# Vision layer on one core: the first two pairs' grey picture summed on VectorE, first transfers divided over two queues, set-up placed later

## The chip, the core and the metric

One core of a Trainium2 chip runs the whole program. The metric is device time in microseconds (us) of one execution. TensorE (PE) does matmuls, VectorE (DVE) and ScalarE (ACT) do elementwise work, GpSimd (POOL) here does little but issue accumulating DMAs, and SyncE (SP) only issues DMAs. Matrices are float32. The profile gives the clock that was granted to TensorE; 1.00 is 2.4 GHz and 0.50 is 1.2 GHz.

## The reference, cut to what matters

64 colour images of 256 x 256 are turned to grey, convolved with two 3 x 3 Scharr filters, and go through one RWKV attention layer (256 channels, 256 time steps) and a layer of 8 experts.

```python
gray = einsum('bchw,c->bhw', x, (0.2989, 0.587, 0.114))
h = (abs(conv(gray, sx)) + abs(conv(gray, sy))) / 2       # padding SAME
n = layernorm(h)                                          # rows are time steps
k, v, r = (mix(n, tm_i) @ W_i.T for i in 'kvr')           # mix: n and n one step before
h = h + (sigmoid(r) * wkv(w, u, k, v)) @ Wo.T             # wkv: a scan over 256 steps
h = h + top1_expert(layernorm(h), Wg, W1, b1, W2, b2)
```

## The kernel before, in words

The images go in 32 pairs through six stages, LOAD, GRAY, EDGE, WKV, PROJ, FFN. Step n of every engine's program holds stage s of pair n - s, so that six pairs are under way. Steps 0 to 7 are written out, a loop of four steps a turn does those from 8 to 31, and steps 32 to 36 drain. Each engine runs its own list in order and waits on semaphores.

The way of a pair to its first matmul is through DRAM. In LOAD, SP brings red and green to `planes` (four DMAs of 256 KB, L265) and copies blue from DRAM to DRAM into `gray_dram` (two DMAs, L273). In GRAY, ACT scales red and green in place (`scaled`, L784), and POOL adds them to `gray_dram` with accumulating DMAs, red first (L405), then green (L411), with a wait for red between. SP waits for green and then loads `rows_in` (ten DMAs, 1.6 MB: for each of two images three shifted copies of the rows on 32 partitions each, L329, and two border rows of 3 partitions each, L335). In EDGE, PE convolves `rows_in` with `conv_w` in four groups (`convolve(0)` to `(3)`, L1002), ACT takes absolute values (L776), DVE sums them (L511) and makes the statistics, ACT normalises (L875), PE transposes (L1096), DVE makes the differences and `mixed_k`, `mixed_v` (L557). In WKV of the next step PE projects to k, v, r (L1008), and DVE and ACT run the scans.

There is one `rows_in`, two `planes`, two images' worth of `gray_dram` for each of two pairs. SP's list in step n is: `planes` of pair n (after green of pair n - 2 has been added), wait for the four convolutions of pair n - 2, blue of pair n, wait for green of pair n - 1, `rows_in` of pair n - 1, then the results of pair n - 5.

PE's list in a step begins with `convolve(0)`, `convolve(1)`, `project_k(0)`, `convolve(2)`, `convolve(3)`, `project_k(1)`. `convolve(2)` waits for the first absolute value of its own pair, since they share a bank. ACT's list in a step begins with the two `scaled` of the next pair, then the absolute values.

Set-up stands ahead of and between the first steps: SP zeroes all of `gray_dram` (1 MB), loads the filter `scharr_dj`, eight small parameter arrays and Wk, Wv, Wr before it loads the first blue; PE transposes parameters and these weights before the first convolution; DVE prepares the first expert layer (`setup_experts`) just ahead of its step 2, the other weights ahead of its step 3.

## Time and profile before

| | us |
|---|---|
| three runs, median | 1195.4 |
| lowest and highest | 1194.34, 1196.62 |
| the profiled execution, its own time | 1192.23 |
| its span | 1190.7 |
| PE busy | 1109.3 (93%) |
| DVE busy | 1003.7 (84%) |
| ACT busy | 858.2 (72%) |

The span runs from the first instruction to the last. A busy share is a mean over stages: here the first stretch and the last differ from the long middle. Rows of the timeline give the start of a merged group, its length, the engine, the line, and in brackets the idle time of the engine ahead of it and what ended that. `SPq` and POOL rows of DMAs are issues, not the movement of data. A view with DMA landings counts from issue to landing.

### The profile page before, as it was taken

The page shows a single profiled execution, that of the slowest core. Times are in us where ns is not written, and L with a number is a line of the kernel's source. Part 1 is how long each engine was busy: PE and PEld are TensorE (multiplying, and loading weights), DVE is VectorE, ACT ScalarE, POOL GpSimd, SP SyncE. Part 2 cuts the span into 40 slices and gives each one's busy share as a digit, 9 for nine tenths or more (in the row PEclk, how much of TensorE's full clock was granted, in tenths as well). Part 3 has the DMA queues.
Part 4 walks back from the last instruction along what each step waited for, and adds up shares of the span by engine and source line. Part 5 has one row for each costly group of instructions (what it writes and reads, how often), then busy time and mean ns, then how long its engine had stood idle before and what let it go on. Part 6 is the DMA issues. An engine that isn't in the chain of part 4 may idle for free.

```text
span 1190.7 us, 16854 instructions
## 1 busy us (share of the span) xinstructions
PE 1109.3 (93%) x5571; PEld 696.7 (59%) x5571; DVE 1003.7 (84%) x1828; ACT 858.2 (72%) x1380; POOL 177.3 (15%) x242
## 2 busy tenths in 40 slices
PE   1277799999999999999999999999999999999997
PEld 0033366666666666656666666656666666666666
DVE  1257999999998999999999999999998999999971
ACT  2046788777777787777777877777778877777652
POOL 5211101111111110111110101111101111110000
PEclk9967899999999999999999999999999999999999
DMA  7997756776676766776767667766766677662001
GB/s 187 207 169 121 133 127 128 149 154 140 136 151 150 139 134 134 158 143 135 147 146 146 132 129 159 153 132 136 158 145 123 137 149 153 141 102 47 18 18 36
DMA packets 164837, 157.79 MB, mean 133 GB/s; under 512 B 12528, under 2 KB 164678, under 8 KB 164678
## 3 DMA queue, kind: packets, MB, share of 16 engines
q1 hardware_dynamic: 129990, 123.84, 42.7%
q0 software_dynamic: 34816, 33.56, 22.3%
q8 instruction: 17, 0.28, 0.1%
q14 instruction: 14, 0.11, 0.0%
HBM read 105.96 MB, written 68.17 MB: 146 GB/s over the span
## 4 chain that ended last, share of the span: by engine, by line
PE 90%; DMA 3%; DVE 3%; ACT 2%; SPq 1%; issue 0%; POOL 0%; POOLq 0%; DVEq 0%
PE bank L1008 28%; PE bank L1144 18%; PE bank L1074 15%; PE bank L1002 10%; PE bank L1050 9%; PE bank L1096 4%; DMA rows_in<-gray_dram 2%; PE bank L1122 2%; PE bank L1145 1%; DMA gray_dram<-planes 1%; PE bank L1087 1%; PE bank L1131 1%; PE bank L1063 1%; SPq L329 1%; DMA scharr_dj<-in_L_tok_scharr_dram 0%
## 5 line engine op out<-in xcount | busy, mean ns | idle before, releaser
L1144 PE MATMUL bank<-w_sb,hidden 128*128 128x256 f32 x1024 | 238.8, 380 | 0.8 <-ACT hidden L860 0.8
L1144 PEld LDWEIGHTS bank<-w_sb,hidden 128*128 128x128 f32 x1024 | 184.6, 190 | 29.2 <-ACT hidden L860 1.5
L1002 PE MATMUL bank<-rows_in,conv_w 102*32 102x512 f32 x1024 | 129.9, 628 | 31.5 <-DMA rows_in<-gray_dram 31.5
L1008 PE MATMUL bank<-mixed_k,w_k_t 128*128 128x512 f32 x256 | 127.5, 622 | 4.1 <-DVE mixed_k L557 4.1
L1008 PE MATMUL bank<-mixed_r,w_r_t 128*128 128x512 f32 x256 | 118.6, 607 | 4.8 <-DVE mixed_r L557 4.8
L1074 PE MATMUL bank<-normed_hi,w_hi 128*128 128x512 f32 x256 | 122.2, 477 | 0.0
L1008 PE MATMUL bank<-mixed_v,w_v_t 128*128 128x512 f32 x256 | 120.1, 592 | 0.0
L568 DVE TENSOR_TENSOR_SCAN max_state<-neg_exp_w,bank 128x256 f32<-128x256 f32 x128 | 80.7, 672 | 45.3 <-PE bank L1008 45.3
L1050 PE MATMUL bank<-w_o_t,rwkv 128*128 128x256 f32 x512 | 117.5, 382 | 0.0
L403 POOL TENSOR_TENSOR pool_turn<-pool_turn 128x1 f32<-128x1 f32 x32 | 7.9, 246 | 663.1 <-ACT planes L784 663.1
L1050 PEld LDWEIGHTS bank<-w_o_t,rwkv 128*128 128x128 f32 x512 | 94.9, 190 | 12.0 <-issue 0.5
L1074 PE MATMUL bank<-normed_lo,w_hi 128*128 128x512 f32 x256 | 100.7, 393 | 0.0
L1074 PE MATMUL bank<-normed_hi,w_lo 128*128 128x512 f32 x256 | 100.2, 391 | 0.0
L852 ACT ACTIVATE route_t<-bank 128x512 bf16<-128x512 bf16 x32 | 19.1, 597 | 103.5 <-PE bank L1063 103.5
L700 DVE TENSOR_TENSOR resid<-bank,resid 128x512 f32<-128x512 f32 x64 | 43.9, 686 | 57.7 <-PE bank L1145 57.7
L1002 PEld LDWEIGHTS bank<-rows_in,conv_w 102*32 102x32 f32 x1024 | 29.8, 113 | 100.6 <-issue 81.2
L1008 PEld LDWEIGHTS bank<-mixed_k,w_k_t 128*128 128x128 f32 x256 | 46.7, 202 | 66.2 <-issue 60.4
L860 ACT ACTIVATE hidden<-bank,b_full 128x512 f32<-128x512 f32 x128 | 81.4, 693 | 3.8 <-PE bank L1074 2.2
L776 ACT ACTIVATE abs_a<-bank 128x512 f32<-128x512 f32 x64 | 37.8, 591 | 63.9 <-PE bank L1002 63.9
L1008 PEld LDWEIGHTS bank<-mixed_r,w_r_t 128*128 128x128 f32 x256 | 49.4, 194 | 57.1 <-issue 48.2
L1096 PE MATMUL bank<-ident,normed 128*128 128x128 f32 x512 | 67.4, 275 | 14.3 <-ACT normed L875 14.3
L1096 PEld LDWEIGHTS bank<-ident,normed 128*128 128x128 f32 x512 | 59.4, 142 | 36.3 <-issue 16.4
(132 smaller groups left out, 2230.5 us busy)
## 6 DMA issues: line engine op xcount, KB each, us to landing
rows_in<-gray_dram SPq DMA_DIRECT2D x192, 256.0 KB
planes<-in_x_dram SPq DMA_DIRECT2D x128, 256.0 KB, 5.0
gray_dram<-planes POOLq DMA_DIRECT2D x128, 256.0 KB, 6.1
gray_dram<-in_x_dram SPq DMA_DIRECT2D x64, 256.0 KB, 6.5
out_dram<-resid SPq DMA_DIRECT2D x64, 256.0 KB, 2.2
rows_in<-gray_dram SPq DMA_DIRECT2D x128, 24.0 KB
gray_dram<-rows_in SPq DMA_DIRECT2D x1, 1032.0 KB
hidden<-in_L_ffn_W_dram SPq DMA_DIRECT2D x2, 256.0 KB, 10.3
```

What stands on the lines that cost most here:

```text
L568: ins = dve.tensor_tensor_scan(max_state[:, 2 * ct + i, 1:T + 1], neg_exp_w[:, ct:ct + 1].to_broadcast([P, T]), bank[BANK_K[ct]][:, i * T: ...
L700: dve.tensor_tensor(total, pair_view(bank[BANK_Y[half]]), total, ALU.add).then_inc(s_result, 1)
L776: act.activation((abs_a[:, half, :], total)[c], bank[BANK_EDGE[n]][:, :], ACT.Abs).then_inc(s_abs, 1)
L852: act.activation(route_t[:, :, :].rearrange("p i t -> p (i t)"), route_ps, ACT.Copy).then_inc(s_route_t, 1)
L860: act.activation(hidden[:, m, :, :], pair_view(bank[BANK_HIDDEN[m]]), ACT.Gelu, bias=b1_full[:, m:m + 1]).then_inc(s_hidden, 1)
L1002: ins = pe.matmul(bank[BANK_EDGE[n]][ROW_TILE * q:ROW_TILE * (q + 1), :], conv_w[0:TAPS, c, :], rows, start=True, stop=True)
L1008: ins = pe.matmul(ps[:, :], w_t[i][:, kt, ct * P:(ct + 1) * P], mixed[i][:, 2 * kt:2 * kt + 2, :].rearrange("p i t -> p (i t)"), start=(kt ...
L1050: ins = pe.matmul(bank[BANK_WO[half]][:, i * D:(i + 1) * D], rwkv[:, 2 * kt + i, half * P:(half + 1) * P], w_t[3][:, kt, :], start=(kt == ...
L1074: ins = pe.matmul(bank[BANK_HIDDEN[m]][:, :], weights[:, kt, m * P:(m + 1) * P], part[:, kt, :, :].rearrange("p i t -> p (i t)"), start=(k ...
L1096: ins = pe.transpose(ps[:, col:col + P], src[:, 2 * half + i, ct * P:(ct + 1) * P], ident[:, :])
L1122: ins = pe.matmul(bank[BANK_LOGITS_T][32 * q:32 * (q + 1), 0:P], wg_t[:, kt, :], normed2_t[:, kt, i, half * P:(half + 1) * P], start=(kt = ...
L1144: pe.matmul(ps, hidden[:, m, i, rows], w2_sb[:, m, :], start=(m == 0), stop=False)
```

## The change

Pairs 0 and 1 no longer go through the accumulating DMAs. SP loads red, green and blue of the first half of the rows of both pairs into SBUF, ACT's queue those of the second half (`load_first`); DVE sums them in four instructions a pair (`first_gray_of`) into `first_gray`, which lies in the second `rows_in`; SP and ACT store a half each (`store_first`) and, after both halves are stored, load an image's rows each (`load_rows`). Only the border rows of `gray_dram` are zeroed. The filter, the parameters and Wr are issued on ACT's queue. From pair 2 on the way is as before (`has_later`), with two `rows_in` in turn and other waits on SP. PE's first work is the convolution; the transposes of parameters and weights come after it in step 2, those of Wo, Wg and b1 in step 3. DVE's parts of the set-up move to step 2 (`setup_projections`), ahead of step 3 (`setup_first_layer`) and ahead of step 4 (`setup_rest`). The line `best_rank<-cap` is gone. Below is the core of the diff. Left out of it are: the removed set-up code of SP, which now stands in ACT's program; the bodies of the row loads, unchanged; the semaphores.

```diff
+FIRST = 2
+CLEARED_B2 = 1
+SETUP_CONV, SETUP_PARAMS, SETUP_PROJECTIONS, SETUP_W1, SETUP_ALL = 5, 6, 10, 14, 24
+PE_PARAMS, PE_PROJECTIONS, PE_EXPERTS = 1, 2, 3
...
-        rows_in = sb("rows_in", [P, TILES, 2, D])
+        rows_in = [sb(f"rows_in{i}", [P, TILES, 2, D]) for i in range(2)]
...
-        zeros = rows_in[:, :, :, :].rearrange("p t i w -> p (t i w)")[:, 0:8 * PITCH]
+        first_flat = rows_in[1][:, :, :, :].rearrange("p t i w -> p (t i w)")
+        first_gray = [first_flat[:, i * NB * PITCH:(i + 1) * NB * PITCH].rearrange("p (b w) -> p b w", b=NB)
+                      for i in range(FIRST)]
+        first_blue = [resid[1 + i] for i in range(FIRST)]
+        zero_rows = first_flat[0:4, 2 * NB * PITCH:2 * NB * PITCH + PITCH]
...
+        def load_first(eng, i, half):
+            for plane, dst in enumerate((planes[i][:, 2 * half:2 * half + 2, 0, :],
+                                         planes[i][:, 2 * half:2 * half + 2, 1, :],
+                                         first_blue[i][:, 2 * half:2 * half + 2, :])):
...
+                eng.dma_start(dst, src.rearrange("n p w -> p n w")).then_inc(first_in[i][half], 16)
+        def store_first(eng, i, half):
+            dst = gray_dram[i, :, 1 + half * P:1 + (half + 1) * P, :].rearrange("i p w -> p i w")
+            eng.wait_ge(s_first_zeros, 1)
+            eng.wait_ge(s_first_gray, HALF * i + half + 1)
+            eng.dma_start(dst, first_gray[i][:, 2 * half:2 * half + 2, :]).then_inc(first_stored[i], 16)
+        def load_rows(eng, buf, i):
...
+            for dj in range(3):
...
+                eng.dma_start(rows_in[buf][ROW_TILE * dj:ROW_TILE * (dj + 1), :, i, :], src
+                              ).then_inc(rows_loaded[buf], 16)
...
+                eng.dma_start(rows_in[buf][first:first + 3, :, i, :], src).then_inc(rows_loaded[buf], 16)
...
-            load_planes(0, 0, 0)
...
-            for src, dst in zip((Wk, Wv, Wr), w_raw):
+            load_first(sp, 0, 0)
+            load_first(sp, 1, 0)
+            store_first(sp, 0, 0)
+            sp.wait_ge(s_borders, 16)
+            sp.wait_ge(first_stored[0], 16 * HALF)
+            load_rows(sp, 0, 0)
+            store_first(sp, 1, 0)
+            for src, dst in zip((Wk, Wv), w_raw):
                 sp.dma_start(dst, src.rearrange("(a p) c -> p a c", p=P)).then_inc(s_w_in, 16)
+            sp.wait_ge(first_stored[1], 16 * HALF)
+            load_rows(sp, 1, 0)
...
-                if at.has(LOAD) and not at.first():
-                    wait(sp, s_green, at.count(LOAD, 16 * HALF, 16 * HALF, back=2))
-                    load_planes(at.j, at.u, at.buf(LOAD))
-                if at.has(LOAD) or at.has(GRAY):
-                    wait(sp, s_edge_ps, at.count(LOAD, 4, 4, back=2))
-                if at.first():
-                    sp.wait_ge(s_borders, 32)
-                if at.has(LOAD):
-                    load_blue(at.j, at.u, at.buf(LOAD))
-                if at.has(GRAY):
+                if at.has_later(LOAD):
+                    b = at.buf(LOAD)
+                    wait(sp, s_green, at.count(LOAD, 16 * HALF, 16 * HALF, back=2 + FIRST))
+                    if at.is_step(2) or at.is_step(3):
+                        sp.wait_ge(s_first_gray, HALF * (at.u - 1))
+                    load_plane(0, at.j, at.u, b)
+                    wait(sp, s_edge_ps, at.count(LOAD, 4, 4, back=3))
+                    load_plane(1, at.j, at.u, b)
+                    wait(sp, rows_loaded[b], at.dma_count(LOAD, X_DMAS, back=2))
+                    load_blue(at.j, at.u, b)
+                if at.has_later(GRAY):
                     b = at.buf(GRAY)
-                    wait(sp, s_green, at.count(GRAY, 16 * HALF, 16 * HALF))
+                    wait(sp, s_green, at.count(GRAY, 16 * HALF, 16 * HALF, back=FIRST))
+                    if not at.has(LOAD):
+                        wait(sp, s_edge_ps, at.count(GRAY, 4, 4, back=2))
                     for i in range(2):
...
+                        load_rows(sp, b, i)
...
+            def first_gray_of(i):
+                for half in range(HALF):
+                    rows = slice(2 * half, 2 * half + 2)
+                    total = first_gray[i][:, rows, 1:D + 1]
+                    dve.wait_ge(first_in[i][half], 48)
+                    dve.scalar_tensor_tensor(out=total, in0=planes[i][:, rows, 0, :],
+                                             scalar=GRAY_WEIGHTS[0] / GRAY_WEIGHTS[2], in1=first_blue[i][:, rows, :],
+                                             op0=ALU.mult, op1=ALU.add).then_inc(s_first_mix, 1)
+                    dve.wait_ge(s_first_mix, HALF * i + half + 1)
+                    dve.scalar_tensor_tensor(out=total, in0=planes[i][:, rows, 1, :],
+                                             scalar=GRAY_WEIGHTS[1] / GRAY_WEIGHTS[2], in1=total,
+                                             op0=ALU.mult, op1=ALU.add).then_inc(s_first_gray, 1)
+            first_gray_of(0)
...
+            first_gray_of(1)
             dve.wait_ge(s_built, 1)
-            done(dve.tensor_copy(best_rank[:, 0:1], cap[:, :]))
-            dve.wait_ge(s_pe_setup, 1)
-            done(dve.tensor_copy(params[:, :], params_ps))
+            done(dve.tensor_copy(ident_bf[:, :], ident[:, :]))
             assert own[0] == SETUP_CONV
...
+                dve.wait_ge(s_pe_setup, PE_PARAMS)
+                done(dve.tensor_copy(params[:, :], params_ps))
...
                 dve.tensor_scalar(cap_less_u[:, :], params[:, ROW_U:ROW_U + CH], -1.0, BONUS_CAP,
                                   ALU.mult, ALU.add)
+                dve.wait_ge(s_pe_setup, PE_PROJECTIONS)
+                for i in range(3):
+                    scale_weights(i, 1.0)
                 dve.wait_ge(s_act_setup, 1)
                 done(dve.tensor_scalar(neg_exp_w[:, :], exp_w[:, :], -1.0, None, ALU.mult))
...
                 assert own[0] == SETUP_PROJECTIONS
...
-            run_steps(dve, step, {2: setup_first, 3: setup_output_projection})
+            run_steps(dve, step, {3: setup_first_layer, 4: setup_rest})
 
 
         @block.scalar
         def _(act):
-            act.wait_ge(s_dve_setup, SETUP_PARAMS)
-            act.activation(exp_w[:, :], params[:, ROW_W:ROW_W + CH], ACT.Exp).then_inc(s_act_setup, 1)
+            load_first(act, 0, 1)
...
+            load_first(act, 1, 1)
+            act.wait_ge(s_first_zeros, 1)
+            act.dma_start(bass.AP(gray_dram.tensor, 0, [[IMAGE, 4], [(T + 1) * PITCH, 2], [1, PITCH]]),
+                          zero_rows.unsqueeze(1).to_broadcast([4, 2, PITCH])).then_inc(s_borders, 16)
+            store_first(act, 0, 1)
+            act.wait_ge(s_borders, 16)
+            act.wait_ge(first_stored[0], 16 * HALF)
+            load_rows(act, 0, 1)
+            store_first(act, 1, 1)
...
+            act.wait_ge(s_cleared, CLEARED_B2)
+            for r, src in rows:
+                act.dma_start(params_raw[r:r + src.shape[0], :], src).then_inc(s_params_in, 16)
+            act.dma_start(w_raw[2], Wr.rearrange("(a p) c -> p a c", p=P)).then_inc(s_w_in, 16)
+            act.wait_ge(first_stored[1], 16 * HALF)
+            load_rows(act, 1, 1)
+            def decay_rate(at):
+                if not at.is_step(EDGE):
+                    return
+                act.wait_ge(s_dve_setup, SETUP_PARAMS)
+                act.activation(exp_w[:, :], params[:, ROW_W:ROW_W + CH], ACT.Exp).then_inc(s_act_setup, 1)
...
+            def setup_experts(at):
+                if not at.is_step(WKV):
+                    return
+                pe.wait_ge(s_v, 1)
                 pe.wait_ge(s_wo_in, 16)
                 transposed_weights(3)
 
+                pe.wait_ge(s_gap, 2)
...
-                    wait(pe, s_rows_loaded, at.count(EDGE, 16 * X_DMAS, 16 * X_DMAS))
+                    b = at.buf(EDGE)
+                    wait(pe, rows_loaded[b], at.dma_count(EDGE, X_DMAS))
...
                 project_r(1, at)
+                setup_experts(at)
                 transpose_normed2(0, at)
                 transpose_normed2(1, at)
                 second_layer(0, at)
+                setup_projections(at)
                 transpose_normed(0, at)
```

SP, from its first DMA to the planes of pair 2, before. `planes` and `gray_dram<-in_x_dram` are colours of a pair, `edge`, `gate`, `bonus`, `hidden`, `w_sb` hold parameters and weights at this time:

```order
L265 DMA planes<-in_x_dram 128x2x256 x4
L277 DMA gray_dram<-rows_in 128x2064
...
L298 DMA gate<-in_L_attn_Wk_dram 128x2x256
...
L273 DMA gray_dram<-in_x_dram 128x2x256 x2
L265 DMA planes<-in_x_dram 128x2x256 x4
L273 DMA gray_dram<-in_x_dram 128x2x256 x2
L329 DMA rows_in<-gray_dram 32x8x256 x3
L335 DMA rows_in<-gray_dram 3x8x256 x2
...
L302 DMA hidden<-in_L_ffn_W_dram 128x8x64 x2
L305 DMA edge<-in_L_ffn_b_dram 8x256 x3
...
L308 DMA w_sb<-in_L_ffn_W_dram 128x4x256
L265 DMA planes<-in_x_dram 128x2x256 x4
```

and now (`resid` holds blue of the first pairs, `gray_dram<-rows_in` is the store of `first_gray`):

```order
L251 DMA planes<-in_x_dram 128x2x256 x2
L251 DMA resid<-in_x_dram 128x2x256
L251 DMA planes<-in_x_dram 128x2x256 x2
L251 DMA resid<-in_x_dram 128x2x256
L258 DMA gray_dram<-rows_in 128x2x258
L266 DMA rows_in<-gray_dram 32x8x256 x3
L272 DMA rows_in<-gray_dram 3x8x256 x2
L258 DMA gray_dram<-rows_in 128x2x258
L324 DMA gate<-in_L_attn_Wk_dram 128x2x256
...
L266 DMA rows_in<-gray_dram 32x8x256 x3
...
L330 DMA hidden<-in_L_ffn_W_dram 128x8x64 x2
...
L306 DMA planes<-in_x_dram 128x2x256 x4
```

The rows of pair 0 now stand behind two sets of loads and one store, those of pair 1 ahead of the expert weights. The planes of pair 2 stay behind all of it, and those of pair 3 come right after.

ACT, the start of its program before:

```order
L756 ACT_TABLE_LOAD
L756 ACTIVATE exp_w<-params 128x2
L906 ACT_TABLE_LOAD
L784 ACTIVATE planes<-planes 128x4x256 x4
L776 ACTIVATE abs_a<-bank 128x512
```

and now:

```order
L251 DMA planes<-in_x_dram 128x2x256 x2
L251 DMA resid<-in_x_dram 128x2x256
L795 DMA scharr_dj<-in_L_tok_scharr_dram 32x6x1 x3
...
L251 DMA planes<-in_x_dram 128x2x256 x2
...
L804 DMA gray_dram<-rows_in 4x2x258
L258 DMA gray_dram<-rows_in 128x2x258
L266 DMA rows_in<-gray_dram 32x8x256 x3
...
L258 DMA gray_dram<-rows_in 128x2x258
...
L820 DMA bonus<-in_L_attn_Wr_dram 128x2x256
L266 DMA rows_in<-gray_dram 32x8x256 x3
...
L978 ACT_TABLE_LOAD
L848 ACTIVATE abs_a<-bank 128x512
```

ACT's first absolute value now stands behind 33 DMA issues of its own queue, and so behind the wait for the store of pair 1.

DVE, between `mixed_v` of pair 1 and the first scan of step 4, before:

```order
L547 TENSOR_TENSOR step_diff<-normed_t 128x1024
L557 SCALAR_TENSOR_TENSOR mixed_k<-step_diff,params,normed_t 128x512 x2
L557 SCALAR_TENSOR_TENSOR mixed_v<-step_diff,params,normed_t 128x512 x2
L568 SCALAR_TENSOR_TENSOR max_state<-neg_exp_w,bank 128x256 x2
L577 TENSOR_TENSOR gap<-bank,max_state 128x512
```

and now:

```order
L594 SCALAR_TENSOR_TENSOR mixed_v<-step_diff,params,normed_t 128x512 x2
L503 TENSOR_SCALAR w_o_t<-bank 128x512
L522 COPY wg_t<-bank 128x2x8
L528 TENSOR_TENSOR b_full<-bank,params 64x1 x8
L534 CAST den_state<-edge 128x256
L535 TENSOR_TENSOR edge<-edge,den_state 128x256
L536 COPY b_parts<-den_state 8x256
L537 CAST den_state<-edge 128x256
L538 COPY b_parts<-den_state 8x256
L539 TENSOR_TENSOR edge<-edge,den_state 128x256
L540 CAST b_parts<-edge 8x256
L605 SCALAR_TENSOR_TENSOR max_state<-neg_exp_w,bank 128x256 x2
```

Ten rows of set-up now stand between them that were ahead of steps 2 and 3.

## Rows read from the trace of the kernel before

**Rows 1.** The page's 40 slices of 29.8 us: PE's busy tenths.

```profile
PE   1277799999999999999999999999999999999997
```

**Rows 2.** What PE waited for over the span: us, times, longest.

```profile
PE bank L1002 <- DMA rows_in<-gray_dram: 31.5, 2, 30.1
```

**Rows 3.** One stretch of the middle: busy us of each engine, clock, DMA share, GB/s.

```profile
300.00:600.00 300.00, 300.00 (x1535) 189.10 (x1534) 273.78 (x502) 236.30 (x380) 45.85 (x54) 1.00 0.70 143
```

**Rows 4.** The timeline from 0 to 60 us: first DMAs to the first convolutions.

```profile
0.82 1.98 SPq L265 DMA_DIRECT2D planes<-in_x_dram  x4
...
3.78 3.39 SPq L281 DMA_DIRECT2D scharr_dj<-in_L_tok_scharr_dram  x3
...
20.88 2.61 POOL L405 DMA_DIRECT2D gray_dram<-planes  x2 [0.30 <-issue]
...
36.12 1.34 SPq L329 DMA_DIRECT2D rows_in<-gray_dram  x3
...
40.32 3.96 SPq L302 DMA_DIRECT2D hidden<-in_L_ffn_W_dram  x2
...
48.92 6.31 PE L1002 MATMUL bank<-rows_in,conv_w 102*32 102x512 f32 x32 [30.12 <-DMA rows_in<-gray_dram]
...
51.77 2.04 SPq L265 DMA_DIRECT2D planes<-in_x_dram  x4
...
55.29 0.60 ACT L776 ACTIVATE edge<-bank 128x512 f32<-128x512 f32 x1 [0.38 <-PE bank L1002]
```

**Rows 5.** Landings: L265 issued at 0.8, L265 at 51.8, L273 at 55.3.

```profile
DMA to landing us min/median/max: 2.8/3.6/6.0
DMA to landing us min/median/max: 4.4/4.7/5.3
DMA to landing us min/median/max: 5.7/5.8/5.9
```

**Rows 6.** The timeline of step 2 to 3: the sums, ACT's scaling, the mix.

```profile
57.74 1.29 DVE L511 TENSOR_TENSOR edge<-edge,abs_a 128x512 f32<-128x512 f32 x2
...
66.30 1.99 ACT L784 ACTIVATE planes<-planes 128x1024 f32<-128x1024 f32 x2
...
67.70 1.41 DVE L557 SCALAR_TENSOR_TENSOR mixed_k<-step_diff,params,normed_t 128x512 f32<-128x512 f32 x2
```

**Rows 7.** The chain of waits in step 3: start, us, what.

```profile
71.84 3.64 PE bank L1002 x16
75.48 3.31 PE bank L1008 x4
...
80.64 1.93 PE bank L1008 x4
```

**Rows 8.** The timeline from the red of pair 2 to step 4.

```profile
69.11 2.40 POOL L405 DMA_DIRECT2D gray_dram<-planes  x2
...
84.75 1.32 SPq L329 DMA_DIRECT2D rows_in<-gray_dram  x3
...
98.31 3.28 PE L1002 MATMUL bank<-rows_in,conv_w 102*32 102x512 f32 x16
...
105.67 3.60 PE L1008 MATMUL bank<-mixed_k,w_k_t 128*128 128x512 f32 x4 [4.09 <-DVE mixed_k L557]
```

**Rows 9.** The chain of waits: first convolutions of step 6.

```profile
170.81 1.72 PE bank L1002 x16
```

**Rows 10.** The timeline in the middle: planes, blue, rows, the next convolution.

```profile
612.35 2.08 SPq L265 DMA_DIRECT2D planes<-in_x_dram  x4
616.21 1.43 SPq L273 DMA_DIRECT2D gray_dram<-in_x_dram  x2
629.28 1.33 SPq L329 DMA_DIRECT2D rows_in<-gray_dram  x3
...
644.20 1.92 PE L1002 MATMUL bank<-rows_in,conv_w 102*32 102x512 f32 x16
```

**Rows 11.** DMA share of 628 to 648, forty slices of 0.5 us, in tenths.

```profile
DMA  9200399999999999999322210094000000000943
```

173 lines of the change are left out of this document (85 added, 88 removed).

## The prediction

> **What bounds the kernel now.** I read the page's slices first. PE is at 9 tenths from the sixth slice to the last but one, and low before [rows 1]. A stretch of the middle shows 300.00 us busy of 300.00 at clock 1.00 [rows 3]: there PE has no idle time at all, so nothing that DMA, DVE or ACT do there shows, unless it comes to be late. Then I read what PE waited for: `rows_in` for 31.5 us in two waits, the longest 30.1 [rows 2], both at the start. From the convolutions of step 6, at 170.81 [rows 9], the steps follow each other at PE's pace. So the change is worth what it brings forward in the start, and the question is how much of a gain at the first convolution is left when PE has become the bound.
>
> Three points carry it: the first convolution, 48.92 [rows 4]; the k projection of step 3, 75.48, with its second half done at 80.64 + 1.93 = 82.57 [rows 7]; the k projection of step 4, 105.67 [rows 8]. From there to 170.81 nothing of the change stands on the path, so the gain at the last of these is the gain of the kernel.
>
> **Pair 0, up to the first convolution.** Removed: the wait for blue, the scaling on ACT, red and green accumulated one after the other (POOL's red at 20.88, the rows issued at 36.12, so 15.2 us [rows 4]), and on SP the 1 MB of zeros and the small arrays ahead. Added: six loads for pair 0, three a queue, the same for pair 1, four DVE sums, a store. Four loads took 1.98 us to issue from 0.82 [rows 4] and landed after 6.0 at most [rows 5]. Six loads over two queues are issued by about 2.3; with half as much data again, and pair 1's beside it, I put the landing at 8.5. A sum of 128 x 512 costs 0.7 (1.41 for two in L557 [rows 6]); with the first half begun earlier, grey is ready at 10. The store of 256 KB a half takes at least 2.8 [rows 5]: 13. The bounds are 11 and 17: on ACT's queue the second half's store stands behind the filter's loads, whose first three took 3.39 to issue [rows 4], and behind pair 1.
>
> Then the rows. Before, from first issue to first convolution 48.92 - 36.12 = 12.8, of which issuing is 4.2, up to the next load's 40.32 [rows 4]. In the middle the same load is issued at 629.28 [rows 10], and the DMA share has fallen to zero by 640.2 [rows 11]: 11. That row also shows how: nine tenths until about 637.5, then 3, 2, 2, 2, 1 for 2.5 us. I take 11, since two queues halve the issue but not the movement; bounds 10 and 12.8. First convolution at 13 + 11 = 24, against 48.92.
>
> Two rules of the Trainium skill bear on it (page "DMA: Bandwidth & Descriptors"). Its section "Issuing engines are not separate DMA queues" says that DMAs of different issuers run on the same 16 engines and that issuing from several saves only the issuing time. By that rule the divided rows gain at most half of the issue, 2.1 us; the sum above takes 12.8 to 11, and by the rule alone it would be 10.7, so the trace and the rule differ by 0.3 us. "Why a DMA increments its semaphore by 16 and not by 1" says that a DMA runs on as many engines as divide its outer dimensions, three for a border load of 3 partitions; that would make the low tail of the row, which a second queue doesn't remove.
>
> **Pair 0, from the convolution to k.** Before, four convolution groups and the last absolute value were done at 55.29 + 0.60 = 55.89 [rows 4], but DVE came to the sums only at 57.74, since it prepared the expert layer first. The second sum, at 58.4, could have begun at 55.9: 2.5 us that the move gives back. Against it, ACT can't take an absolute value before its queue is issued, and that waits for the store of pair 1. This store stands behind the rows of pair 0 in the same queues, so about 25.5; then half of 4.2 for the rows of pair 1: ACT is free at 27.6, and I allow it 1.4 to load its function table. `convolve(2)` waits for the first absolute value, 29.6; two groups 3.6 (as the 3.64 [rows 7]), last absolute value at 33.7, the sum 0.7. From the end of the sums to the end of `mixed_k` took 67.70 + 1.41 - 57.74 - 1.29 = 10.1 [rows 6]: 44.5. PE's transposes of weights, DVE's `setup_projections` (three copies of 128 x 512, 0.7 each as in L557, and small ones) and ACT's exponential fit beside ACT's normalising and PE's transposes, if Wk, Wv and Wr have landed by 33; they are issued before 22, behind rows of pair 0. The convolutions of pair 1 need its rows: issued at 25.5, with weights of 0.75 MB ahead, they land at 38.5, before PE has done its transposes at 41; 3.64 more, and k of step 3 starts at 44.7. The gain here is 75.48 - 44.7 = 30.8.
>
> **Pair 2, which still goes the old way.** Its planes stand on SP behind the rows of pair 1 and the expert weights. Before, that stretch ran from 40.32 to 51.77, 11.5 us, and ended 2.9 after rows had landed [rows 4]; I take rows landed plus 2.9, so 41.4 (by 11.5 after the issue it is 39). Four issues are 2.0, landing 4.7 to 5.3 [rows 5]: 48.2. Blue is issued 1.2 later and takes 5.8 [rows 5]: 50. ACT's list in step 3 begins with scaling these planes, 1.99 [rows 6], so the absolute value that `convolve(2)` waits for comes at 50.8 instead of 48: k's second half is done at 50.8 + 1.9 + 1.93 = 54.6, a gain of 28.0 against 82.57.
>
> POOL issues red at 50.4. Before, from red to the issue of rows 84.75 - 69.11 = 15.6, and to the convolution 98.31 - 69.11 = 29.2 [rows 8]; but that convolution stood behind PE's transposes, and by the 11 of the middle the rows could have been there after 26.6. I take 27.5, nearer to 26.6, because the other loads come earlier and interfere less. Rows at 77.9, two convolutions 3.3 to 3.6 [rows 7, 8], k of step 4 at 81.4. By the other path, DVE and ACT's scans, k of step 4 was ready 105.67 - 82.57 = 23.1 after k of step 3: 54.6 + 23.1 = 77.7. **The rows of pair 2 are last**, by 3.7 us, where before the wait was for `mixed_k` [rows 8]. The gain is 105.67 - 81.4 = 24.3.
>
> **Set-up on DVE and PE.** `setup_first_layer` has two products of 128 x 512 and two passes of 128 x 1024, by the 0.7 of L557 [rows 6] at most 4.2 us of DVE, beside PE's first k projection of step 3, 3.31 [rows 7]. `setup_rest` has one copy of 128 x 512 and smaller ones, an estimate of 4 to 5; it lies beside the wait of 3.7 for pair 2's rows and the 3.60 of k [rows 8]. If that wait goes, 0.5 to 2.5 of it shows, since before DVE had only the 3.60 there. PE's part in step 3 stands where PE waits for ACT's normalised values, ahead of DVE's scans, which end later. I cost all three at nothing here. Two `rows_in` matter only where rows are early; in the middle the convolution comes at 644.20, 4.0 after the last data [rows 10, 11], so they bring nothing there.
>
> **Sum.** On the profiled execution 1192.2 - 24.3 = 1167.9. The median of the runs is 3.2 above that execution, and I take the gain from it: 1195.4 - 24.3 = 1171.1, say 1171.0.
>
> **The rivals.**
>
> *A, forecast: rows of pair 2 last, 1171.0.* With the bounds of its terms (26.6 to 29.2; first stretch 11 to 17; rows 10 to 12.8) it reaches from 1167.5 to 1176. Chance 0.50.
>
> *B, the old path keeps up.* If accumulating DMAs with less beside them take 24 instead of 27.5, or the planes land 3 to 4 earlier because the divided rows leave SP's queue less full, the scans bind. Then k of step 4 is at 75 to 77.7, a gain of 28 to 30.7: 1166. For it: rows landed 11 after issue in the middle. Against: 29.2 was the time that the trace shows. Chance 0.18.
>
> *C, the start is crowded.* Twelve loads of 256 KB, the filter's tiny pieces and stores on two queues take 4 us longer, or SP is held on its issues, as L302 was for 3.96 [rows 4], with the planes of pair 2 still behind. ACT then stands at the scaling, with the absolute values behind it. 6 us more: 1177. Chance 0.21.
>
> *D, slower: rows late in the loop.* SP now sends blue of a pair right after its planes, 616.21 - 612.35 - 2.08 = 1.8 us earlier than before [rows 10], beside POOL's red. If that makes green and so rows later than the 4.0 of slack, every one of the 28 steps from 6 to 33 pays. At 0.87 us a step the 24.3 are gone, so from 4.9 us later; at 5.5, 1171 + 28 x 1.5 = 1213. Against it: the bytes are the same, and a start 1.8 earlier hardly makes the end 5 later. Chance 0.07.
>
> *E, no difference.* ACT's queue holds ACT, or a store or border row lands so late that pair 1 or 2 arrives at about the old time: a loss of 22 to 27 us on the estimate, about 1195. Chance 0.04.
>
> **The numbers.** A run of this kernel can tell about 0.2%, 2.4 us, from no change. Faster has A, B and C: 0.89; same has E: 0.04; slower D: 0.07. The range for 8 in 10 takes A and B whole and most of C: 1164 to 1180.
>
> **What would show it.** The first convolution at 22 to 28; a gap in PE between `convolve(1)` and `convolve(2)` of step 2, ended by ACT; the k projection of step 3 near 45; in step 3 the absolute values behind a wait of ACT for `planes`; in step 4 PE waiting for `rows_in` and not for `mixed_k`, with k near 81; steps in the middle as long as before, with PE busy 300.00 of 300.00. A first convolution past 30, planes of pair 2 issued past 45, or any wait of PE for `rows_in` past step 5 would make the prediction wrong.

## The result and the profile of the changed kernel

The changed kernel takes 1180.8 us (median of 4 runs, 1175.6 to 1182.9) beside 1194.9 for the kernel before (4 runs). The ratio is 0.9875, 95% interval 0.9839 to 0.9911. So it is faster by 1.25%, and not by the 2.0% of the forecast: 1171.0 was 9.8 us too low, and the median lies 0.8 us outside the range of 1164 to 1180. The profiled execution took 1175.57 us, the fastest of the four, with a span of 1173.8 against 1190.7 before: 16.9 us less.

PE's busy tenths, against [rows 1], and what PE waited for, against [rows 2] (us, times, longest):

```profile
PE   0567999999999999999999999999999999999997
...
PE bank L1087 <- DMA rows_in<-gray_dram: 38.2, 2, 33.0
...
PE bank L1087 <- ACT abs_a L848: 5.3, 2, 3.5
```

PE waits for `rows_in` longer than before, 38.2 us against 31.5, and yet the kernel is faster. The first wait starts at 0 now, because the transposes of parameters and weights no longer stand ahead of it. The second, 38.2 - 33.0 = 5.2 us, is new: it stands in step 4. Code lines have moved: L1087 is the convolution, L1093 the projections, L251 `load_first`, L258 `store_first`, L266 and L272 `load_rows`, L306 and L314 planes and blue on SP, L429 and L435 POOL's red and green, L848 ACT's absolute values, L856 its scaling of planes.

The timeline of the start (start us, us, engine, line; in brackets the idle time ahead and what ended it), to be laid beside [rows 4]:

```profile
2.40 1.82 ACTq L795 DMA_DIRECT2D scharr_dj<-in_L_tok_scharr_dram  x3
...
6.14 1.80 ACTq L251 DMA_DIRECT2D resid<-in_x_dram  x1
7.62 0.69 DVE L458 SCALAR_TENSOR_TENSOR rows_in<-planes,resid 128x512 f32<-128x512 f32 x1 [7.62 <-DMA resid<-in_x_dram]
7.98 3.62 ACTq L804 DMA_DIRECT2D gray_dram<-rows_in  x1
...
10.38 0.98 DVE L462 SCALAR_TENSOR_TENSOR rows_in<-planes,rows_in 128x512 f32<-128x512 f32 x1
11.70 1.45 ACTq L258 DMA_DIRECT2D gray_dram<-rows_in  x1
16.45 0.17 DVE L469 TENSOR_SCALAR scharr_dj<-scharr_dj 102x6 f32<-102x6 f32 x1 [5.09 <-DMA scharr_dj<-in_L_tok_scharr_dram]
19.93 1.32 SPq L266 DMA_DIRECT2D rows_in<-gray_dram  x3
...
32.97 2.79 PE L1087 MATMUL bank<-rows_in,conv_w 102*32 102x512 f32 x12 [32.97 <-DMA rows_in<-gray_dram]
34.08 1.31 SPq L266 DMA_DIRECT2D rows_in<-gray_dram  x3
```

The chain of waits of the same stretch names the two stores (start, us, what):

```profile
11.70 8.16 DMA gray_dram<-rows_in
...
22.41 11.65 DMA gray_dram<-rows_in
```

Grey is ready at 11.36, the store issued at 11.7 lands at 19.9, the rows are in at 32.97. Then SP's queue and pair 2, in steps 2 to 4, against [rows 6 to 8]:

```profile
36.39 4.01 SPq L330 DMA_DIRECT2D hidden<-in_L_ffn_W_dram  x2
40.44 7.50 SPq L333 DMA_DIRECT2D edge<-in_L_ffn_b_dram  x3
49.25 2.04 SPq L306 DMA_DIRECT2D planes<-in_x_dram  x4
53.12 1.99 PE L1093 MATMUL bank<-mixed_k,w_k_t 128*128 128x512 f32 x4 [0.37 <-DVE mixed_k L594]
56.07 2.00 ACT L856 ACTIVATE planes<-planes 128x1024 f32<-128x1024 f32 x2 [5.78 <-DMA planes<-in_x_dram]
58.61 3.35 PE L1087 MATMUL bank<-rows_in,conv_w 102*32 102x512 f32 x16 [3.50 <-ACT abs_a L848]
58.71 2.61 POOL L429 DMA_DIRECT2D gray_dram<-planes  x2
72.57 1.33 SPq L266 DMA_DIRECT2D rows_in<-gray_dram  x3
85.44 3.64 PE L1087 MATMUL bank<-rows_in,conv_w 102*32 102x512 f32 x16 [5.23 <-DMA rows_in<-gray_dram]
89.01 2.30 PE L1093 MATMUL bank<-mixed_k,w_k_t 128*128 128x512 f32 x4
...
152.20 1.90 PE L1087 MATMUL bank<-rows_in,conv_w 102*32 102x512 f32 x16
```

PE's wait of 5.23 for `rows_in` isn't what sets step 4, though. The chain of waits that ends in DVE's first scan of step 4 doesn't run through these rows at all, but through the planes of pair 2, ACT's scaling of them and DVE:

```profile
50.81 5.18 DMA planes<-in_x_dram
...
64.14 1.28 DVE max_state L605 x2
...
87.17 1.33 DVE mixed_v L594 x2
...
93.12 1.28 DVE max_state L605 x2
```

ACT scales the planes ahead of the absolute value that `convolve(2)` of step 3 waits for; so the second half of k of step 3 ends only at 64.10, and DVE's second scan of that step begins at 64.14. From there the scans, `mixed_k`, `mixed_v` and, from 88.41, the set-up of `setup_rest` follow on DVE and ACT without a wait for a DMA, up to 93.12. The first half of k of step 4 was done at 91.31. So the rows of pair 2 could have come 1.8 us later and the scan would have begun at the same time. So it is the first scan of step 4, more than PE's k, that is to be followed through the runs, as the table at the end of the experiments does. It was at 109.31 before: a lead of 16.2.

The lead over the kernel before at each marker, beside the forecast:

| | before | after | lead | forecast |
|---|---|---|---|---|
| first convolution | 48.92 | 32.97 | 16.0 | 24.9 |
| k of step 3 | 75.48 | 53.12 | 22.4 | 30.8 |
| k of step 4 | 105.67 | 89.01 | 16.7 | 24.3 |
| step 6 (first convolution of a pair) | 170.62 | 152.20 | 18.4 | 24.3 |
| last convolution of the loop | 1083.82 | 1065.42 | 18.4 | 24.3 |
| span | 1190.7 | 1173.8 | 16.9 | 24.3 |

From step 6 to the last convolution nothing is gained or lost. The lead grows by 1.7 us between k of step 4 and step 6 and shrinks by 1.5 behind the loop. The granted clock, which has a section below, differs in both stretches: from 120 to 150 us it was 1.00 now and 0.83 before, from 1130 to 1150 it was 0.91 now and 1.00 before.

### The profile page after: what moved, and what is told of

Its sections match the earlier page's. It is cut to its first block, busy times and chain, and to the rows that moved or that the text cites. A ratio compares the mean times of both kernels' runs of the same rounds, so it can differ in the third digit from the quotient of the medians.

```text
span 1173.8 us, 16855 instructions
## 1 busy us (share of the span) xinstructions
PE 1102.8 (94%) x5571; PEld 693.1 (59%) x5571; DVE 1009.1 (86%) x1835; ACT 853.2 (73%) x1375; POOL 166.5 (14%) x234
## 4 chain that ended last, share of the span: by engine, by line
PE 89%; DVE 4%; DMA 2%; ACT 2%; SPq 1%; ACTq 1%; issue 0%; DVEq 0%
PE bank L1093 27%; PE bank L1229 19%; PE bank L1159 16%; PE bank L1135 9%; PE bank L1087 9%; PE bank L1181 4%; DMA gray_dram<-rows_in 2%; PE bank L1207 1%; PE bank L1230 1%; PE bank L1172 1%; PE bank L1216 1%; PE bank L1148 1%; SPq L333 1%; DMA planes<-in_x_dram 0%; DVE max_state L605 0%
## 5 line engine op out<-in xcount | busy, mean ns | idle before, releaser
L1229 PEld LDWEIGHTS bank<-w_sb,hidden 128*128 128x128 f32 x1024 | 184.9, 191 | 28.9 <-ACT hidden L932 1.5
L1087 PE MATMUL bank<-rows_in,conv_w 102*32 102x512 f32 x1024 | 130.6, 629 | 44.5 <-DMA rows_in<-gray_dram 38.2
L1093 PE MATMUL bank<-mixed_k,w_k_t 128*128 128x512 f32 x256 | 124.3, 609 | 0.4 <-DVE mixed_k L594 0.4
L1093 PE MATMUL bank<-mixed_r,w_r_t 128*128 128x512 f32 x256 | 116.9, 600 | 5.9 <-DVE mixed_r L594 5.9
L1093 PE MATMUL bank<-mixed_v,w_v_t 128*128 128x512 f32 x256 | 120.1, 592 | 0.0
L1087 PEld LDWEIGHTS bank<-rows_in,conv_w 102*32 102x32 f32 x1024 | 29.6, 113 | 113.4 <-issue 81.8
L1093 PEld LDWEIGHTS bank<-mixed_r,w_r_t 128*128 128x128 f32 x256 | 48.9, 192 | 56.8 <-issue 46.9
L1093 PEld LDWEIGHTS bank<-mixed_k,w_k_t 128*128 128x128 f32 x256 | 45.7, 198 | 61.5 <-issue 58.8
L1093 PEld LDWEIGHTS bank<-mixed_v,w_v_t 128*128 128x128 f32 x256 | 48.5, 189 | 49.0 <-issue 46.4
L1181 PEld LDWEIGHTS bank<-ident,normed 128*128 128x128 f32 x512 | 59.1, 141 | 30.1 <-issue 16.5
```

Of the source, the lines that this page charges most:

```text
L1087: ins = pe.matmul(bank[BANK_EDGE[n]][ROW_TILE * q:ROW_TILE * (q + 1), :], conv_w[0:TAPS, c, :], rows, start=True, stop=True)
L1093: ins = pe.matmul(ps[:, :], w_t[i][:, kt, ct * P:(ct + 1) * P], mixed[i][:, 2 * kt:2 * kt + 2, :].rearrange("p i t -> p (i t)"), start=(kt ...
L1181: ins = pe.transpose(ps[:, col:col + P], src[:, 2 * half + i, ct * P:(ct + 1) * P], ident[:, :])
L1229: pe.matmul(ps, hidden[:, m, i, rows], w2_sb[:, m, :], start=(m == 0), stop=False)
```

## Experiments

Each variant stands on the changed kernel. The kernels of a group ran on one chip beside the same runs of the kernel before; groups are compared by their ratio to it. One thousandth is 1.2 us.

### The start and SP's queue

**again** is the changed kernel once more, unedited.

> The changed kernel once more, to see the spread of its runs. Its profiled execution took 1175.6 us at a mean granted clock of 0.990, three others 1179.9 to 1182.9 at 0.983 to 0.984. Theory clock: the runs differ in how long TensorE is granted 0.50 in the first 150 us, while the DMAs and the first convolution (33 us) stay where they are; a run of this kernel near 1180 shows about twice the half-clock time there. Theory DMA: the slower runs have the first convolution or the rows of pair 2 later by 4 to 7 us, at the same clock.

1179.3 us (1177.2 to 1180.4), ratio 0.9890 (0.9875 to 0.9905). The profiled execution has its DMA marks within 1 us of those above (first convolution 32.83, k at 52.14 and 90.00), but step 6 only at 155.01, and a span of 1178.0. That is the theory of the clock: from 30 to 150 us TensorE was at the lower level for 37.2 us here and for 20.4 in the execution above, 1.8 times as long. It is one pair of executions.

**weights_late** moves the expert weights, which stand ahead of the planes of pair 2 on SP, behind them:

```diff
-            run_steps(sp, step, {2: load_later_weights})
+            run_steps(sp, step, {3: load_later_weights})
```

> One line of SP: the expert weights, b2, Wo, Wg and W2 are issued ahead of its step 3 instead of step 2, so behind the planes and blue of pair 2. In the changed kernel SP was held on W1 and b2 from 36.4 to 48.0, the planes of pair 2 were issued at 49.25, and ACT waited for them 5.8 us. Theory queue: the planes go out at 36.4, ACT's wait goes, the second half of k of step 3 ends near 57 to 59 instead of 64.1, k of step 4 starts near 83 instead of 89.0, and the kernel is 5 to 7 us faster. Rival weights: the first expert layer's weights then come after 54, DVE waits for them ahead of step 3, and SP is held on b2 with the planes of pair 3 behind it: 0 to 2 us faster.

1174.6 us (1173.7 to 1175.0), ratio 0.9854 (0.9839 to 0.9869): 4.6 us under *again*. The planes are issued at 36.20 instead of 49.25, ACT waits for them 0.76 instead of 5.78, and `convolve(2)` doesn't wait. Its timeline, from there to step 4:

```profile
36.20 2.03 SPq L306 DMA_DIRECT2D planes<-in_x_dram  x4
51.36 2.01 ACT L856 ACTIVATE planes<-planes 128x1024 f32<-128x1024 f32 x2 [0.76 <-DMA planes<-in_x_dram]
54.03 2.86 POOL L429 DMA_DIRECT2D gray_dram<-planes  x2
64.77 0.18 POOL L433 TENSOR_TENSOR pool_turn<-pool_turn 128x1 f32<-128x1 f32 x1 [7.87 <-DMA gray_dram<-planes]
...
84.62 3.64 PE L1087 MATMUL bank<-rows_in,conv_w 102*32 102x512 f32 x16 [8.10 <-DMA rows_in<-gray_dram]
```

13 us at the issue are 4.7 at POOL's red, since ACT scales only after step 3's normalising, and 0.8 at the convolution of step 4: red is now issued beside the weights, and POOL waits 7.87 for its landing instead of 4.37. k of step 4 starts at 88.19, 0.8 us before that of the changed kernel's first profile and 1.8 before *again*'s; step 6 starts at 149.95, 2.3 and 5.1 before. But neither of these markers shows what was won. Without ACT's wait, k's second half of step 3 is done at 59.17, DVE's second scan of that step begins at 60.58 (65.20 in *again*), `mixed_k` of step 4 at 82.19 (86.81), and the first scan of step 4 at 90.63 (94.17): 3.5 us earlier. Now DVE waits 1.12 us for k there, so that the rows of pair 2 have become last; without that wait the scan could have begun up to 1.1 earlier. The rest of the 5.1 at step 6 goes with the granted clock (below).

**filter_few** replaces the three loads of single 4-byte elements, 576 of them, by one of 96 runs of 72 bytes, from which DVE picks its columns:

```diff
-            for dj in range(3):
-                act.dma_start(scharr_dj[ROW_TILE * dj:ROW_TILE * (dj + 1), :],
-                              bass.AP(scharr.tensor, dj, [[0, ROW_TILE], [3, 6], [1, 1]]),
...
+            act.dma_start(scharr_all[0:3 * ROW_TILE, :], bass.AP(scharr.tensor, 0, [[0, 3 * ROW_TILE], [1, 18]])
...
```

> The filter comes by one DMA of 96 runs of 72 bytes (the 18 values to 96 partitions) and the two border loads of before, instead of three DMAs of 192 runs of 4 bytes each; DVE picks each third value while scaling. In the changed kernel the filter landed at 16.45, the zero borders took 3.6 us to issue behind it, the second half of the first grey picture was stored from 11.7 to 19.9, and the first convolution came at 33.0. Theory filter: its tiny pieces hold ACT's queue; without them the filter lands before 12, the store by 15 to 16, the first convolution comes at 28 to 29, and the kernel is 3 to 5 us faster. Rival crowd: the 3 MB of picture ahead of the store take that time anyway; the first convolution moves by under 1.5 us, and so does the kernel.

1175.8 us (1173.5 to 1177.5), ratio 0.9859 (0.9843 to 0.9874): 3.5 us under *again*. Border, second store and rows on ACT's queue, and the first convolution:

```profile
5.36 0.38 ACTq L807 DMA_DIRECT2D gray_dram<-rows_in  x1
...
11.41 0.38 ACTq L259 DMA_DIRECT2D gray_dram<-rows_in  x1
15.82 1.36 ACTq L267 DMA_DIRECT2D rows_in<-gray_dram  x3
...
28.73 3.64 PE L1090 MATMUL bank<-rows_in,conv_w 102*32 102x512 f32 x16 [28.73 <-DMA rows_in<-gray_dram]
```

The border is issued in 0.38 instead of 3.62 us, DVE doesn't wait for the filter, the second store lands after 4.4 instead of 8.2, and the first convolution is 4.2 us earlier. The first scan of step 4 is 2.5 us before *again*'s, and the kernel as a whole 3.5.

**pair1_late** leaves the filter and moves pair 1's loads instead, on both queues:

```diff
-            load_first(sp, 1, 0)
             store_first(sp, 0, 0)
+            load_first(sp, 1, 0)
...
-            load_first(act, 1, 1)
...
             store_first(act, 0, 1)
+            load_first(act, 1, 1)
```

> The changed kernel with the three planes of pair 1 issued behind the stores of pair 0 on both queues, instead of ahead of them. Theory of the queue's order (the 256 KB store of pair 0 took 7.8 to 8.2 us because pair 1's 1.5 MB stood ahead of it): the store lands 3 to 5 us after its issue at 9.4 to 11.7, the rows of pair 0 are issued by 16 instead of 19.9, the first convolution runs at 28 to 30 instead of 33.0, k of step 3 and of step 4 follow by the same 3 to 5 us, and the kernel is 2.5 to 5 us faster than the changed one (1174 to 1177). Rival (the filter's 576 small pieces, still ahead of ACT's half of the store, and the issue times on ACT hold it): the store of the second half lands at 17 or later all the same, the first convolution stays past 31 and the kernel within 1.5 us of the changed one. Second rival (pair 1 comes late instead): the first convolution is earlier, but that of step 2 waits for its rows by as much, and k of step 3 at 52 to 53 does not move.

1176.7 us (1174.6 to 1178.0), ratio 0.9872 (0.9853 to 0.9890). The place is right: the store issued at 11.36 has landed at 16.36, after 5.0.

```profile
11.36 0.40 ACTq L258 DMA_DIRECT2D gray_dram<-rows_in  x1
...
16.36 1.33 SPq L266 DMA_DIRECT2D rows_in<-gray_dram  x3
...
29.84 3.61 PE L1087 MATMUL bank<-rows_in,conv_w 102*32 102x512 f32 x16 [29.84 <-DMA rows_in<-gray_dram]
```

The size is at the low end: the first convolution is 3.1 us earlier, the first scan of step 4 is 2.6 before *again*'s, the kernel about 2, and by the intervals this could be nothing. Here DVE waited for the filter until 12.52, not 16.45: the same 576 pieces land 4 us earlier when pair 1 isn't beside them. So either alone, the filter's pieces or pair 1's loads, leaves the store at 4.4 to 5.0 us, and only both together bring it to 8.2: taking away either brings the rows' issue to about 16.

**one_queue** issues all of the start's transfers on SP, in the same order.

```diff
             load_first(sp, 0, 0)
+            load_first(sp, 0, 1)
...
             load_rows(sp, 0, 0)
+            load_rows(sp, 0, 1)
```

> The changed kernel with all first transfers on SP's queue, ACT's in their order merged in; ACT issues no DMA. It undoes the division over two queues alone. By issue times alone the first convolution comes later by the issues that no longer run side by side: about 3 for the loads, 0.5 for the store, 2.1 for the rows, so 4 to 6 us, and the weights and planes of pair 2 stand behind 8 more parameter loads (2.5 us). Against it, ACT takes its first absolute value at once instead of behind its queue (1.8 us of PE idle in step 2). Theory issue: 3 to 7 us slower than the changed kernel. Rival shared engines: what bounds the start is the data, which the division doesn't move faster: within 2 us of the changed kernel, or faster.

1179.5 us (1176.9 to 1182.3), ratio 0.9901 (0.9887 to 0.9914), 0.2 us from *again*: the division over two queues is worth nothing that can be measured. The rows are issued over 4.1 us from 21.19 instead of over 2.4 from 19.93, and are there at 33.05 and 32.97:

```profile
21.19 1.31 SPq L266 DMA_DIRECT2D rows_in<-gray_dram  x3
...
33.05 6.44 PE L1082 MATMUL bank<-rows_in,conv_w 102*32 102x512 f32 x32 [33.05 <-DMA rows_in<-gray_dram]
```

Two effects lie in the whole kernel's time, since ACT no longer stands at its issues until 36.4: `mixed_k` of step 3 is 1.05 us earlier than in *again* (49.62 and 50.67). It doesn't reach step 4, where the first scans are at 94.10 and 94.17.

### The other parts of the change

**one_rows** goes back to a single tile for the rows; pair 1's then wait for the first pair's convolutions (and are issued by SP alone).

```diff
-                eng.dma_start(rows_in[buf][ROW_TILE * dj:ROW_TILE * (dj + 1), :, i, :], src
+                eng.dma_start(rows_in[0][ROW_TILE * dj:ROW_TILE * (dj + 1), :, i, :], src
...
+            sp.wait_ge(s_edge_ps, 4)
             load_rows(sp, 1, 0)
+            load_rows(sp, 1, 1)
```

> The changed kernel with one tile for the rows again: every pair's rows go to the first tile, pair 1's are loaded by SP only after the four convolutions of pair 0, and SP's wait stands ahead of blue as in the kernel before; the second tile only holds the first grey pictures. It undoes the two tiles alone. The convolutions of pair 0 ended at 42.0, so the rows of pair 1 are issued then instead of at 34.1 and land at 53 to 55 instead of 47; the convolutions of pair 1 come 4 to 5 us later, and everything behind on SP 8 us. Theory tiles: 4 to 8 us slower than the changed kernel. Rival: ACT is freed from its last rows, pair 2 binds by its accumulating DMAs, and the loss is under 2 us.

1183.3 us (1181.6 to 1185.4), ratio 0.9924 (0.9907 to 0.9941), 3.4 thousandths or 4 us above *again*. Pair 1's rows are issued at 38.07 instead of 34.08, PE waits for them 4.83, and SP's list is shifted behind them: planes of pair 2 at 52.36. The first scan of step 4 is 3.25 us after *again*'s, and from step 6 to the end both take 1023 us. So the two tiles brought about 4 us, all in the start; the two ran on different chips, and their intervals nearly touch.

**proj_back** puts one piece of set-up back ahead of the first convolution: PE's transposes of the parameters and of Wk, Wv, Wr, with DVE's copies and ACT's exponential.

```diff
+            pe.wait_ge(s_params_in, 16 * 8)
+            pe.transpose(params_ps, params_raw, ident[0:ROWS, 0:ROWS]).then_inc(s_pe_setup, 1)
+            pe.wait_ge(s_w_in, 48)
+            for i in range(3):
+                ins = transposed_weights(i)
```

> The changed kernel with one piece of the set-up put back where it was: TensorE's transposes of the parameters and of Wk, Wv and Wr, VectorE's copies of them and ScalarE's exponential stand ahead of the first convolution again instead of in the step behind. Theory (this part of the change is worth what the weights' landing is late against the rows): the weights land at 30 to 37 in the trace of the changed kernel and the rows at 33, so the first convolution goes to 33 to 38 and the kernel is 0 to 5 us slower (1180 to 1185). Rival (it is worth nothing, since ScalarE's table load and the rows come as late as before): within 1 us. That it is faster by over 1.5 us would say that the moved work stands in a worse place now, in DVE's and PE's step behind the first convolution, where k of step 3 is waited for.

1178.0 us (1177.4 to 1181.6), ratio 0.9889 (0.9869 to 0.9909): nothing. And that although PE sits until the last weight has landed:

```profile
37.98 1.97 PE L1027 MATMUL bank<-ident,gate 128*128 128x128 f32 x8 [1.32 <-DMA bonus<-in_L_attn_Wr_dram]
40.73 4.86 PE L1081 MATMUL bank<-rows_in,conv_w 102*32 102x512 f32 x32
...
60.53 1.92 PE L1081 MATMUL bank<-rows_in,conv_w 102*32 102x512 f32 x16 [1.43 <-ACT abs_a L846]
...
87.84 3.64 PE L1081 MATMUL bank<-rows_in,conv_w 102*32 102x512 f32 x16 [7.66 <-DMA rows_in<-gray_dram]
```

The first convolution is 7.8 us later (40.73 against 32.97), k of step 3 is 4.0 later, its second half 0.5 (62.39 against 61.89): the wait for ACT's absolute value, behind the planes of pair 2, swallows the rest. Pair 2's own way goes over SP's queue, and that doesn't wait for PE there. The first scan of step 4 is at 94.98, 0.8 us after *again*'s, and here DVE waits 1.62 us for k and so for the rows of pair 2. Once pair 2 sets the end, by its planes or by its rows, an earlier first convolution is worth little by itself.

**b2_gap** moves DVE's seven small instructions on b2 from `setup_rest`, ahead of step 4, into step 3, where DVE waits. In the changed kernel they end at 93.08 and the scan behind them starts about 1.8 us late.

```diff
-                dve.wait_ge(s_b2_in, 48)
...
+                setup_b2(at)
                 den_scan(at)
```

> The changed kernel with the seven b2 instructions of DVE's setup_rest moved from ahead of step 4 into step 3, ahead of the scan of the denominator, where DVE waited 0.8 us for ACT and 3.1 us before that. In the changed kernel setup_rest ran from 88.41 to 93.08, while k of step 4 had its first half done at 91.3, so the first scan started 1.8 us late. Theory path: the scan of step 4 starts at once, 1.5 to 2 us of the kernel. Rival hidden: the later waits of step 4 (mixed_r, normalised values) take it up, or the gap in step 3 isn't free, and the kernel is within 0.5 us of the changed one.

1180.6 us (1176.8 to 1183.7), ratio 0.9903 (0.9880 to 0.9927): no gain. The trace shows why; first ACT's decay, for which the scan L625 waits in the changed kernel, then DVE with the last of the seven, whose first began at 75.60, and that scan:

```profile
75.40 1.04 ACT L893 ACTIVATE decay<-decay 128x1024 f32<-128x1024 f32 x1
...
77.67 0.28 DVE L530 CAST b_parts<-edge 8x256 bf16<-8x256 f32 x1
77.99 2.30 DVE L625 TENSOR_TENSOR_SCAN den_state<-decay,fresh 128x1028 f32<-128x1028 f32 x1
```

The gap in front of that scan was only 0.79 us long, and the seven take 2.4. The scan could begin at 76.44 and begins at 77.99, 1.5 late, and `mixed_k` of step 4 with it. From `mixed_k` to the first scan of step 4 it is then 5.0 us instead of 7.4. So one place gives 2.4 back and the other takes 1.5; the 0.9 that are left are less than the spread (here DVE's second scan of step 3, ahead of the moved work, was already 1.5 later than in *again*).

### Put together

**early2** sends the planes of pair 2 even before pair 1's rows, blue behind them, and lets ACT scale them in step 2; the weights come late as in *weights_late*.

```diff
             store_first(sp, 1, 0)
+            load_plane(0, 0, 2, 0)
+            load_plane(1, 0, 2, 0)
...
-            run_steps(sp, step, {2: load_later_weights})
+            run_steps(sp, step, {3: load_later_weights})
```

> The changed kernel with pair 2 brought forward: its planes are issued behind the first store of pair 1, ahead of its rows, its blue right behind the rows of pair 1, the expert weights ahead of step 3, and ACT scales its planes in step 2 behind the absolute values, where ACT waited 2.6 us, instead of at the head of step 3. Theory pair 2: what binds step 4 is the way of pair 2 through the accumulating DMAs. Red goes out at 46 to 49 instead of 58.7, rows of pair 2 land by 76, k of step 4 is set by the scans and starts near 82 instead of 89; 6 to 8 us faster than the changed kernel, 2 to 3 faster than with the weights late alone. Rival crowd: the planes ahead of the rows of pair 1 hold those up by 3 us, step 3 starts later by as much, and it is no better than with the weights late alone (4.6 us faster).

1175.3 us (1174.3 to 1178.9), ratio 0.9862 (0.9842 to 0.9882): no better than *weights_late*. PE now waits 2.73 for pair 1's rows, k of step 3 is at 56.05, and red is issued at 54.48 as in *weights_late*, since blue stands behind pair 1's rows. The transfers only changed places.

**best1** has early2, filter_few and b2_gap together, and pair 1's rows all on SP.

> The moves of filter_few, b2_gap and early2 together, with all rows of pair 1 on SP's queue, so that ACT isn't held by its queue until 36.4. If the terms add (filter 3.5 as measured, pair 2 6 to 8, b2 1.5, ACT's queue 1.8) it is 12 to 14 us faster than the changed kernel, at 1165 to 1167. If one path takes over (PE between the convolutions of pair 0 and the mix of step 3, which none of the moves shortens) they don't add: 8 to 10 us.

1170.5 us (1169.5 to 1173.3), ratio 0.9822 (0.9803 to 0.9841): 8 us under *again* by the ratios, as much as *filter_few* (3.7) and *weights_late* (4.3) together. Its red and its wait in step 4:

```profile
48.26 2.60 POOL L436 DMA_DIRECT2D gray_dram<-planes  x2
...
80.51 3.64 PE L1103 MATMUL bank<-rows_in,conv_w 102*32 102x512 f32 x16 [7.92 <-DMA rows_in<-gray_dram]
```

Red is 10.4 us earlier than in the changed kernel, but the way from there to the convolution takes 32.3 us instead of 26.7. So two more were tried: **best2** adds *pair1_late*, and **best3** also turns SP's step 3 round, rows of pair 2 ahead of planes and blue of pair 3.

```diff
+                for part in ((gray_part, load_part) if at.is_step(3) else (load_part, gray_part)):
+                    part()
```

> best1 (filter in one DMA, b2's seven instructions a step earlier, rows of pair 1 on one queue, planes of pair 2 ahead of pair 1's rows, later weights a step later) with the planes of pair 1 issued behind the stores of pair 0. If the queue's order at the start still costs there: the first convolution at 25 to 27 instead of 29.3 and 2 to 4 us under best1 (1166.5 to 1168.5). Rival (pair 2's own way sets the end: red scaled at 48.3, convolution at 80.5): the first convolution is earlier, the convolution of step 4 is not, and the kernel is within 1 us of best1.

> best2 with SyncE's step 3 turned round: the rows of pair 2 are issued ahead of the planes and the blue of pair 3, so that less runs beside the stores and the rows of pair 2. In best1 the red of pair 2 was scaled at 48.3 and its rows were used at 80.5, 32 us later, against 26.7 in the changed kernel. Theory (load beside them stretches these transfers): 26 to 28 us between the two, the convolution of step 4 3 to 5 us earlier, the kernel 2 to 5 us under best2. Rival (the way is long by the number of its steps and the two waits on the Pool engine): within 1 us of best2, or slower by 1 to 4 us where the planes of pair 3 come late and ScalarE waits for them in step 4.

1171.0 us (ratio 0.9820, 0.9804 to 0.9836) and 1170.7 us (0.9821, 0.9805 to 0.9837): both as *best1*. In *best2* the first convolution is at 30.53, not at the 25 to 27 expected: the store lands at about 16 with the small filter alone, and pair 1 later only makes the rest later. In *best3* the theory of the load beside holds in part: red 49.30 to convolution 78.23 is 28.9 us, against 30.4 in *best2*, and not the 26 to 28 expected. But the next wait is there at once:

```profile
78.23 3.64 PE L1109 MATMUL bank<-rows_in,conv_w 102*32 102x512 f32 x16 [3.70 <-DMA rows_in<-gray_dram]
83.37 3.78 PE L1115 MATMUL bank<-mixed_k,w_k_t 128*128 128x512 f32 x4 [1.50 <-DVE mixed_k L615]
```

The rows are ready 2.5 us earlier than in *best2* (1.0 of it since red goes out earlier), k of step 4 starts 0.9 earlier (83.37 against 84.31), and it waits for `mixed_k`, so for the scans of step 3. There both ways of the start end together, and shortening one is no longer enough. All three carry *b2_gap*, whose 1.5 us lie on just this second way; *best3* without it wasn't run. And the sign that was named for the rival came too: ACT waits 3.83 us for the planes of pair 3 in step 4, and the second scan of that step begins at 91.91, 0.8 after *best2*'s, though its first began 0.2 earlier.

Over all runs, the first scan of step 4 goes along with the time of the kernel, where the first convolution doesn't (one profiled execution each):

| | first convolution | first scan of step 4 | DVE's wait just ahead of it | step 6 | ratio |
|---|---|---|---|---|---|
| changed kernel | 32.97 | 93.12 | none | 152.20 | 0.9875 |
| *again* | 32.83 | 94.17 | none | 155.01 | 0.9890 |
| *one_rows* | 32.20 | 97.42 | none | 158.45 | 0.9924 |
| *proj_back* | 40.73 | 94.98 | k, 1.62 | 156.15 | 0.9889 |
| *b2_gap* | 33.35 | 94.74 | none | 153.79 | 0.9903 |
| *one_queue* | 33.05 | 94.10 | k, 0.36 | 155.16 | 0.9901 |
| *early2* | 32.58 | 91.87 | none | 152.87 | 0.9862 |
| *filter_few* | 28.73 | 91.65 | none | 152.57 | 0.9859 |
| *pair1_late* | 29.84 | 91.54 | k, 0.34 | 151.23 | 0.9872 |
| *weights_late* | 32.82 | 90.63 | k, 1.12 | 149.95 | 0.9854 |
| *best2* | 30.53 | 87.47 | none | 146.53 | 0.9820 |
| *best3* | 29.48 | 87.26 | k, 0.42 | 149.52 | 0.9821 |
| *best1* | 29.27 | 86.17 | k, 2.15 | 145.50 | 0.9822 |

"None" means that DVE came to the scan from its own list.

## Why the prediction found the places of the path and was short in its size

**What held.** The places of the path, one by one. ACT ends the gap between `convolve(1)` and `convolve(2)` of step 2, 1.76. The absolute values of step 3 stand behind a wait of ACT for `planes`, 5.78. In step 4 PE waits for `rows_in`, 5.23, and not for `mixed_k`, as *the rows of pair 2 are last* said; but by 1.8 us instead of 3.7 (k began at 89.01, `mixed_k` was done at 87.17), and for DVE's scan they were not last at all (see below). The middle is untouched: PE has no wait for rows past step 5, and the lead is 18.4 both at step 6 and at the last convolution, so rival D is out. The spans between the markers came out too:

- first convolution to k of step 3: forecast 20.7, measured 20.2;
- pair 1's rows issued to planes of pair 2 issued: 15.9 and 15.2, though I named only W1 (4.0) and measured that b2's three small loads take 7.50 in that stretch;
- red to the convolution of step 4: 27.5 and 26.7, and this one by luck. The forecast took 15.6 to the issue of the rows and about 11 to 12 from there; measured were 13.9 and 12.9. It had taken the 29.2 of before as partly a wait behind PE's transposes, but there the weights of that convolution waited 0.19 us for `rows_in`, up to 98.30, when the transposes were just ending: the rows themselves had taken until then.

That the divided rows bring little was right as well. The Trainium skill's page "DMA: Bandwidth & Descriptors", section "Issuing engines are not separate DMA queues", says that issuing from several engines saves the issuing time alone; by *one_queue* the trace agrees, and even that is not seen: 1.7 us less of issuing, 0.1 us at the convolution. No run separates the border rows' loads from the others, so what the forecast said of the low tail of the rows' load stays untested. Set-up at nothing held for PE's part (*proj_back*).

**What failed: two terms ahead of the first convolution.** "Stored at 13" was 19.9, 6.9 late. Of this, grey came 1.4 later than the 10 of the forecast, and the store took 8.6 from there instead of 3. The 3 were the 2.8 of [rows 5], the least landing of a load in an empty queue; here the store stood behind 1.5 MB of pair 1 and 576 single elements of the filter. The forecast had named both as the reason for a bound of 17, and yet taken the other end. *filter_few* and *pair1_late* show that each alone is worth 3.6 to 4.1 us at this point, that they are not additive, and that no run came below about 16: none came near the bottom bound, 11. "Rows 11" was 13.0, 0.2 over its upper bound; it is 12.9 and 13.5 in *filter_few* and *pair1_late*. The 11 came from the middle. There the engines moved 1.7 MB between 629.0 and 640.2 (149 GB/s), hardly more than the rows themselves; between 20 and 33 us of the changed kernel they moved 2.8 MB (219 GB/s), since the stores of pair 1, the parameters and the weights are issued right behind the rows. The nearer row was the 12.8 of the start.

Together 8.9 us, and every marker behind is late by about that: the planes of pair 2 by 7.9 (49.25 against 41.4), red by 8.3, the convolution of step 4 by 7.5, its k by 7.6. This is rival C by its mechanism, with 9 us at its head instead of the 4 to 6 given for it. Two of the three signs named for a wrong prediction came, a first convolution past 30 and planes issued past 45; the third, a wait for `rows_in` past step 5, didn't. That SP is held on its issues, the other half of C, was in the forecast's 15.9 already, so it explains none of the shortfall; but *weights_late* shows that it costs 4.6 us, which the forecast had not seen as something to be won.

**What failed as well: the other path, and set-up at nothing.** The forecast had k's second half of step 3 done at 54.6; it was 64.10, 9.5 late. 7.9 of it are the planes'. The rest is mostly clock: it had taken 1.9 for the two convolutions and 1.93 for k, and they took 3.35 and 2.2 (granted clock 0.55 from 58.6 to 62.0). The 23.1 from there to `mixed_k` of step 4 was right (87.17 - 64.10). Then came `setup_rest`, 88.41 to 93.08 on DVE, priced at nothing because it was to lie beside the wait for pair 2's rows and k. That cover ended at 91.31, so 1.8 of it show; the price given for the case that the cover goes was 0.5 to 2.5. So "from there to 170.81 nothing of the change stands on the path" didn't hold. At the first scan of step 4 the lead is 16.2, where k had 16.7.

**What was not costed: two tiles.** The forecast said they bring nothing in the middle, which holds, and matter only where rows are early. By *one_rows* they are worth about 4 us in the start. The sum has them in it without saying so: it issues pair 1's rows at 25.5, ahead of pair 0's convolutions, which one tile doesn't allow.

**The rest.** 24.3 - 7.6 = 16.7 is the gain at k of step 4 in the profiled execution, and 16.9 that of its span; the medians differ by 14.1. The profiled execution is the fastest of the four and has the highest mean clock, 0.990 against 0.983 and 0.984. I had taken the gain from a median as if the changed kernel spread no more than the one before. Of the 9.8 us between forecast and median, 7.4 are in the profiled span (24.3 against 16.9) and the rest is this.

## The granted clock of the start

Two windows of 30 us of the changed kernel (busy us of each engine, then PE's granted clock as a share of 2.4 GHz, where the lower level, 1.2 GHz, counts half; DMA share, GB/s):

```profile
90.00:120.00 30.00, 21.92 (x105) 10.53 (x103) 29.08 (x57) 20.71 (x35) 2.58 (x3) 0.94 0.76 141
120.00:150.00 30.00, 30.00 (x137) 19.36 (x134) 28.77 (x54) 23.54 (x40) 5.19 (x6) 1.00 0.58 100
```

and the same kernel once more, *again*:

```profile
90.00:120.00 30.00, 22.93 (x108) 10.97 (x104) 28.96 (x61) 21.82 (x36) 2.59 (x3) 0.90 0.80 144
120.00:150.00 30.00, 29.40 (x120) 17.43 (x117) 27.18 (x52) 20.76 (x36) 6.22 (x6) 0.92 0.59 92
```

A clock of 0.90 over 30 us means that 6.0 us of it were at the lower level. From 90 to 150 that is 3.6 us in the one execution (0.94 and 1.00) of the changed kernel, 10.8 in the other, with k of step 4 at 89.01 and 90.00; from there to step 6 the first takes 63.2 us and the second 65.0. The same goes through the variants: 61.4, 62.2 and 61.8 us in *best1*, *best2* and *weights_late* with 3.6 at the lower level, 65.1 in *filter_few* with 10.8, 66.2 in *best3* with 10.2. From the first scan of step 4 to step 6 it is 59.1 to 59.3 us in the five executions with 3.0 to 3.6 at the lower level and 59.7 to 61.2 in those with 8.4 to 15.0, but for *best3*, 62.3. So *best3* starts k of step 4 first of all and comes to step 6 3.0 us behind *best2*; 1.0 of that is there at `mixed_k` of step 5, behind ACT's wait for the planes of pair 3 and a k that took 3.78 us where *best2*'s took 2.65; the rest comes later. This share changes from one execution to the next with the same program and nearly the same DMA marks; it goes with a part of the spread of the changed kernel, 1175.6 to 1182.9, not with all: executions at 0.983 and 0.984 took from 1179.9 to 1182.9. For the kernel before it explains nothing: its runs at a mean clock of 0.968 and at 0.981 took the same 1191 to 1193 us. What decides it is left open; no run here was made for it.

## To carry to other kernels

At the start of a kernel, cost a transfer by what stands ahead of it in its queue and beside it on the engines, and take its duration from the start's own rows, not from an empty queue or from the middle. When a first wait is shortened, follow each of the next pairs' transfers down the issuing queue: here 13 us of weights and biases that nobody needed yet stood ahead of the planes that set the end. Count small transfers in pieces as well as in bytes: 576 elements of 4 bytes, 2.3 KB, cost this kernel 3.5 us. And follow a wait on to what it delays: the longest wait of PE in step 4 was for rows that were 1.8 us early for the scan behind it.

## What the runs showed of the hardware that was not expected

- Three loads of b2, 24 KB in all, held SP 7.50 us at their issue behind W1 (4.01), with the planes of pair 2 behind them (L333 above). In *weights_late*, where planes and blue stand ahead of it, W1 itself took 7.80 to issue, b2 3.15 and blue 3.96: with the order, the hold fell on other issues. What sets it, no run here shows.
- The border's zeros, one DMA, took 3.62 us to issue behind the filter's single elements and pair 1's loads, and 0.38 in *filter_few*.
- Two queues in place of one made no difference to when the same rows were in SBUF (32.97 and 33.05), though the last was issued at about 22.3 on two and at 25.3 on one.
